# A spline convolution's chunk spread: two broadcast products, or one tensor-scalar product per mask column

## What is computed

```python
basis, idx = spline_basis(pseudo)          # 8 corner weights of 125 per edge
h = elu(spline_conv(ones, row, col, basis, idx, stn1_w, stn1_b))   # 1 -> 64
h = elu(spline_conv(h,    row, col, basis, idx, stn2_w, stn2_b))   # 64 -> 64
t = elu(h @ stn3_w + stn3_b) @ stn4_w + stn4_b                     # 64 -> 3
new_pseudo = clip(pseudo + t[col] - t[row], 0, 1)
basis2, idx2 = spline_basis(new_pseudo)
x = x + spline_conv(x, row, col, basis2, idx2, conv_w, conv_b)     # 32 -> 32
# spline_conv: out[i] = mean over edges e of node i of  sum_k basis[e,k] * (x[col[e]] @ W[k])  + b
```

## Time and profile before

| | |
|---|---|
| median of 3 runs | 7320.52 us (7303.47 to 7342.39) |
| profiled execution | 7357.94 us, its span 7355.8 us |
| attention with second convolution | 2114 to 3885 us of the span |
| last convolution `p_3` | 5585 to 7300 us |
| busy over the span | PE 63%, DVE 57%, POOL 60%, ACT 22% |
| granted TensorE clock | 0.855 over the span |

### The profile page before, as it was taken

One profiled execution on the slowest core, in us unless ns is written; L12 is line 12 of the kernel. 1 busy time (PEld: TensorE's weight loads), 2 busy tenths in 40 slices (PEclk: granted clock), 3 DMA queues, 4 the chain that ended last, 5 costly groups with the idle time before them and its releaser, 6 DMA issues. The chain is left out here.

```text
span 7355.8 us, 95916 instructions
## 1 busy us (share of the span) xinstructions
PE 4635.6 (63%) x31067; PEld 3408.4 (46%) x31067; DVE 4183.0 (57%) x9381; ACT 1654.2 (22%) x2811; POOL 4443.2 (60%) x4319
## 2 busy tenths in 40 slices
PE   5444442876638888888554667999992444544433
PEld 4444442655536666665443434555552333333322
DVE  7555553769946666666442316777773445444433
ACT  1111120117824444444231000000000222222211
POOL 2777776000057777777433256777764777777763
PEclk9999999569979999999776788999996777777766
DMA  4222221013332222224866581111111111111385
GB/s 73 78 71 78 71 78 26 21 36 151 160 76 54 52 53 53 54 52 49 37 30 180 195 270 39 38 37 37 37 34 23 19 18 18 19 19 18 17 14 14
DMA packets 388448, 441.47 MB, mean 60 GB/s; under 512 B 241139, under 2 KB 312320, under 8 KB 387981
## 3 DMA queue, kind: packets, MB, share of 16 engines
q0 software_dynamic: 137696, 130.26, 18.3%
q1 hardware_dynamic: 191113, 286.63, 12.4%
q10 hardware_dynamic: 59568, 23.69, 1.4%
HBM read 358.46 MB, written 82.34 MB: 60 GB/s over the span
## 5 line engine op out<-in xcount | busy, mean ns | idle before, releaser
L951 POOL DMA_INDIRECT at_far<-att_table,at_rec x1184 | 1227.7, 1037 | 886.0 <-DMA at_rec<-rec_r 400.9
L1524 POOL DMA_INDIRECT p_far<-table,p_rec x1184 | 1242.1, 1049 | 488.2 <-issue 359.9
L2162 PE MATMUL g_l_ps_sum<-g_l_row,g_l_of 128*128 128x392 f32 x3224 | 1062.9, 493 | 19.4 <-DVE g_l_of L2113 19.4
L534 POOL DMA_INDIRECT rec_r<-so_r_rec,so_r_place x806 | 835.0, 1036 | 245.5 <-issue 245.5
L2084 POOL DMA_INDIRECT g_l_got<-table,g_l_index x806 | 811.1, 1006 | 245.5 <-issue 228.4
L2162 PEld LDWEIGHTS g_l_ps_sum<-g_l_row,g_l_of 128*128 128x128 f32 x3224 | 613.2, 190 | 469.7 <-DVE g_l_of L2113 20.6
L1422 PE MATMUL p_ps_outer<-p_spread,p_basis 128*25 128x40 f32 (+1 forms) x4736 | 758.9, 341 | 77.9 <-DVE p_spread L1367 53.1
L1422 PEld LDWEIGHTS p_ps_outer<-p_spread,p_basis 128*25 128x25 f32 (+1 forms) x4736 | 636.0, 183 | 207.6 <-issue 94.5
L1422 PE MATMUL at_bank<-p_spread,p_basis 64*125 64x256 f32 x4736 | 629.3, 418 | 107.1 <-ACT p_outer L1477 107.1
L2096 DVE TENSOR_SCALAR g_l_row<-g_l_iota,edge_row 128x784 f32<-128x784 f32 x806 | 500.3, 693 | 222.2 <-PE g_l_ps_sum L2162 222.0
L489 PE MATMUL so_r_look<-so_r_table,so_r_lo_t 128*128 128x26 f32 x1612 | 425.0, 433 | 310.8 <-DVE so_r_table L433 310.8
(11 more groups left out here) (457 smaller groups left out, 6201.2 us busy)
## 6 DMA issues: line engine op xcount, KB each, us to landing
adjacent<-ad_by_chunk SPq DMA_DIRECT2D x74, 800.0 KB, 3.3
so_r_row<-pad_src SPq DMA_DIRECT2D x62, 832.0 KB, 6.2
g_l_counts<-adjacent SPq DMA_DIRECT2D x60, 800.0 KB, 6.9
g_l1d_counts<-adjacent SPq DMA_DIRECT2D x59, 800.0 KB, 7.1
so_r_low<-pad_lo_src SPq DMA_DIRECT2D x62, 416.0 KB, 4.7
at_far<-att_table,at_rec POOLq DMA_INDIRECT x1184
p_far<-table,p_rec POOLq DMA_INDIRECT x1184
rec_r<-so_r_rec,so_r_place POOLq DMA_INDIRECT x806, 2.1
```

The lines of the kernel that those rows point to most:

```text
L534: pool.indirect_dma_start(out=o.rec[:, :], out_offset=bass.IndirectOffsetOnAxis(ap=place[b][:, j:j + 1], axis=0), in_=rec[b][:, j, :], in_ ...
L951: pool.indirect_dma_start(out=far[b][:, t, :], out_offset=None, in_=g.att_table[:, :], in_offset=bass.IndirectOffsetOnAxis(ap=rec[b][:, t, ...
L1524: pool.indirect_dma_start(out=sl.far[b][:, t, :], out_offset=None, in_=table[:, :], in_offset=bass.IndirectOffsetOnAxis(ap=sl.rec[b][:, t, ...
L2162: last = nc.tensor.matmul(ps_sum[k][:], of4[b][:, j, :, :].rearrange("p k f -> p (k f)"), row1[b][:, j, k * COLS:(k + 1) * COLS], start=Fa ...
```

## The change

```diff
         self.HT = TB // 2
-        self.PT = 4
+        self.PT = 2
...
-            half = self.XT // 2
-            bh = [P, half, self.J, self.CR]
-            for k in range(2):
-                rows = self.far[b][:, s * self.XT + k * half:s * self.XT + (k + 1) * half, self.col:self.col + self.fin]
-                last = nc.vector.tensor_mul(self.spread_to[s % 2][:, k * half:(k + 1) * half, :, :], rows.unsqueeze(3).to_broadcast(bh),
-                                            self.mask[:].unsqueeze(1).unsqueeze(1).to_broadcast(bh))
+
+            rows = self.far[b][:, s * self.XT:(s + 1) * self.XT, self.col:self.col + self.fin]
+            for q in range(self.CR):
+                last = nc.vector.tensor_scalar(self.spread_to[s % 2][:, :, :, q], rows, self.mask[:, q:q + 1], None, ALU.mult)
             last.then_inc(self.spreads, 1)
```

## The result

The changed kernel takes 7396.72 us (median of 7, 7363.94 to 7412.37), the kernel before 7328.02 us in 7 runs. The ratio is 1.0089, with a 95% interval of 1.0071 to 1.0107. So it is slower by 69 us, where a gain of 49 us was forecast and the range ended at 7365. The runs of the experiments fall into seven groups, each with the kernel before beside it: in two groups the kernel before took 7329 and 7337 us, in the other five the same program took 9352 to 9442 us, so a time is compared only with the kernel before of its own group.

What follows compares the result with a forecast made beforehand. POOL's gathers were taken to pace `p_3`: 53 us gained over 31 blocks, 4 lost at the end, so 7357.9 - 53 + 4 = 7309 us profiled, or 7320.5 - 49 = 7272 against the median; range 7222 to 7365.

Steps and rivals of the forecast that it cites:

- What bounds `p_3`: First 31 blocks of `p_3`: POOL paces at 1.357 us a gather, 43.4 us for 32; DVE's own work hides.
- The excess of 3.5 us a block: `p_3`: gathers take 0.11 us over the undisturbed 0.94, through overlapping DVE instructions; some 110 us over 31 blocks.
- The basis pieces: `p_3`: basis in 16 pieces of 250 instead of 8 of 500; gathers lose 0.7 us a block, down from 1.0.
- The spread in `p_3`: `p_3`: eight short instructions a step, each delaying a gather only until its own end; loss 1.0 us a block, from 2.4.
- rival A: Tensor-scalar instructions don't disturb gathers at all: 80 us gained, 7240 us; chance 0.13.
- Rival B: A gather is held until a whole spread step's run has ended: -10 to +35 us, 7310 to 7355; chance 0.25.
- D: DVE gets too slow, PE waits in the attention stage, 43 us more and upwards there: 7310 to 7380; chance 0.07.
- Rival C's deciding point: `p_3`: above 0.215 us an instruction DVE has no pause and gathers starve, 310 to 370 us, 7630 to 7690; chance 0.15.
- The attention stage: POOL isn't the pace there and DVE's waits cover longer steps, so no cost; without the basis's cover 22 us.
- The Trainium skill's rule: Two-port vector instructions and GpSimd exclude each other from a shared port pair, so eight tensor-scalar instructions would be worse than two.

Runs made afterwards that it cites:

- the dense kernel: Changed kernel with dense spread output, PE's products stored column after column and reordered by ACT's copy: 7240.78 us, ratio 0.987 to the kernel before.
- by column: Changed kernel with its spread as two-input tensor-tensor products, same spaced output: 7256.75 us, ratio 0.991 to the kernel before (1.032 to 1.037 in slow groups).
- the second pair: Later profiles of the unchanged kernel before and changed kernel: 17 us lost in `p_3`, 45 in the attention stage, spans 39 us apart.
- basis only: Kernel before with only the basis products cut into pieces of two tiles: 9572, 9611, 9625 and 9584 us, ratios 1.021, 1.023, 1.019, 1.025.

## Why the prediction was wrong

**What bounds `p_3`: right.** POOL paces its first 31 blocks, and the block distance follows the mean of a gather: the dense kernel's 0.967 us gives (0.967 + 0.305) x 32 = 40.7 us, and 40.8 were measured. The excess of 3.5 us a block was the whole prize: the dense kernel took 87 us of `p_3`'s 109 and 96 us of the time. (The two spread products of a step before stood 0.61 us apart from start to start, not 0.65 as the forecast reads them; nothing rests on that.)

**The basis pieces: right in kind, too small.** Forecast was 0.7 us of excess left for a block, from 1.0. Measured: 0.28 (8.7 / 31), from 0.91, so 20 us of `p_3`'s excess gone instead of 9. Whether the kernel gains that by the pieces alone was not measured where POOL sets the pace.

**The spread in `p_3`: the step that failed.** It was "If a gather waits only for the short instruction then running, it loses at most 0.2 us and on average half", with 1.0 us a block as its value. Measured: 4.2 us a block (130.9 / 31), up from 2.5. A gather that is held is not held by an instruction but by the run of them, and it is released 0.12 us after the run's or the step's end (128 of those that met a step in `p_3`; 110 others passed and lost nothing). The premise is true in `p_3` of two-input products (by column: 20.9 us in all, never over 0.14 at once) and of dense one-input products (9.8 us). In `p_3` it is false only of the combination that the change makes, one input and spaced output. I had the row for it and a dense one against it, named the spacing as their difference in rival A, and still took the value next to the dense row.

**Rival B was the mechanism, and was priced for `p_3` alone.** It had a gather held until the end of a step's run. That is what the timelines show, though not for each step: in `p_3` 128 of the 248 steps of 31 blocks held one. Its -10 to +35 us are what `p_3` lost (35 us over 30 blocks, 17 in the second pair); that the whole kernel came out above 7365 is due to the attention stage, which no sum of the forecast charged with a loss but D's. Rival C's deciding point held in the other sense: instructions start 0.196 us apart (a step of eight takes 1.71 us and its last instruction 0.34: 1.37 / 7), under 0.215, so DVE kept a pause after every step or two and no gather starved for 10 us.

**The attention stage: the second error.** "I cost this stage at nothing" rested on POOL's wait of 1.2 us for a block. I only asked what *shorter* gathers would give there. The same row says what longer ones cost: everything beyond 1.2 us. The excess grew by 2.1 us a block (96.8 to 162.5 us in 31 blocks), POOL's wait went to nothing, and the blocks came 1.2 us later each: 35 us, and 45 in the second pair. Half of the loss or more is here. That DVE has room for its steps was right (it still waits 125.8 us for PE), and beside the point.

**The Trainium skill's rule** on the shared port pair ("SBUF — State Buffer", section "SBUF: two separate sides") called the direction. Its unit, the instruction, is not what the runs show: where a gather is held, the seams between instructions of a run don't release it, and a run of the same instruction with dense output doesn't hold it.

## What to carry to other kernels

Where GpSimd's indirect DMAs pace a loop, DVE's time is not the only thing to count: look at what each kind of DVE instruction does to a gather that overlaps it, by comparing the ends of the two. Cutting DVE's work into small pieces helps only if the pieces release the gather; here one-input products with side-by-side output do, two-input products do in `p_3` but less so in the attention stage, and one-input products with spaced output are worse than the big products they replace. When an engine has slack, write it down as a number with its sign: it covers a loss up to that size and no further.

## What was not expected of the hardware

* A run of one-input tensor-scalar products whose outputs are 16 or 32 bytes apart held a `DMA_INDIRECT` until some 0.12 us after the end of the run or step, for up to 2.6 us more than its 0.94, or else gave way and let it pass in 0.94 or 0.95. Dense output: at most 0.24 us in `p_3` and 0.57 in the attention stage. Two-input products with the same spacing: at most 0.14 in `p_3`; but in the attention stage, with 256 elements each, 63 us in all, and in two cases 1.22 and 1.29 us, each until 0.69 us behind the end of a whole step of four, so they aren't free either.
* A single gather of the attention stage took 5.87 us in the second profile of the changed kernel, and one 4.71 us in that of tensor-tensor by column, beside basis pieces. One in 992 costs little; what held them was not found.
* A tensor-scalar product of 128 elements showed 0.35 us with spaced and 0.30 us with dense output, but both start 0.196 to 0.20 us apart.
* PE took 0.61 to 0.62 us for a matmul whose moving operand has a step of 128 or 256 bytes, 0.41 for a dense one (attention stage, same group). ACT copied 512 columns from PSUM in 0.76 us in either order in the attention stage (0.761 before, 0.756 with the reordering copy).
* Where the kernel before took 9355 to 9442 us, "basis only" was 1.9 to 2.5% slower than it, in four groups, with gathers out of the way. Neither the cause of that was found, nor why the same program takes 7330 us in some groups and over 9350 in others.
